# A block of gated delta rule and SwiGLU on one core: seven-product gate and up projections

## The reference

```python
x = x + ga * attn(layernorm(x) * (1 + ca) + sa)
h = layernorm(x) * (1 + cb) + sb
gate = einsum('bsd,hd->bsh', h, w_gate)      # hidden 2048
up = einsum('bsd,hd->bsh', h, w_up)
x = x + gb * einsum('bsh,dh->bsd', silu(gate) * up, w_down)
```

## Time and profile before

| | us |
|---|---|
| median of 3 runs (lowest, highest) | 1060.18 (1058.08, 1065.53) |
| the profiled execution | 1063.38 |
| its span | 1061.6 |
| TensorE busy (share) | 1022.6 (96%) |
| recurrence, about | 425 to 506 |
| feed-forward, about | 509 to 1059 |

### The profile page before, as it was taken

One profiled execution on the slowest core, in us unless ns is written; L12 is line 12 of the kernel. 1 busy time (PEld: TensorE's weight loads), 2 busy tenths in 40 slices (PEclk: granted clock), 3 DMA queues, 4 the chain that ended last, 5 costly groups with the idle time before them and its releaser, 6 DMA issues.

```text
span 1061.6 us, 20179 instructions
## 1 busy us (share of the span) xinstructions
PE 1022.6 (96%) x8112; PEld 822.1 (77%) x8112; DVE 626.2 (59%) x997; ACT 375.0 (35%) x685; POOL 225.8 (21%) x178
## 2 busy tenths in 40 slices
PE   6999999999998999998899999999999999999998
PEld 4676777777676888887777887888888888888886
DVE  5977377899855787878664333343333334334366
ACT  3676674445445343333453112211212212112110
POOL 1322530022025555554301000000000000004191
PEclk9999999999999999999999999999999999999999
DMA  6604336838256666775520001010100101001223
GB/s 212 196 14 135 73 80 165 247 100 215 64 125 170 141 153 146 188 187 130 174 72 28 1 1 60 1 60 1 33 28 1 60 1 58 2 0 70 80 80 119
DMA packets 153438, 97.42 MB, mean 92 GB/s; under 512 B 93569, under 2 KB 130689, under 8 KB 153217
## 3 DMA queue, kind: packets, MB, share of 16 engines
q1 hardware_dynamic: 153344, 96.12, 32.9%
HBM read 64.64 MB, written 31.46 MB: 91 GB/s over the span
## 4 chain that ended last, share of the span: by engine, by line
PE 73%; DVE 10%; DMA 5%; issue 4%; ACT 4%; SPq 4%; POOL 0%; DVEq 0%; ACTq 0%
PE ps L1302 70%; ACT t L1665 3%; PE ps L1310 3%; DVE t L1936 2%; DVE t L2046 2%; DMA scrU<-t 2%; SPq L1179 1%; DVE t L2034 1%; PE ps L1539 1%; DVE t L1941 1%; DVE t L2146 1%; DVE t L1946 1%; DMA scrA<-t 1%; SPq L1239 1%; DMA t<-scrA 1%
## 5 line engine op out<-in xcount | busy, mean ns | idle before, releaser
L1302 PE MATMUL ps<-t,t 128*128 128x512 f32 (+6 forms) x7292 | 969.7, 325 | 30.4 <-DVE t L1936 8.5
L1302 PEld LDWEIGHTS ps<-t,t 128*128 128x128 f32 (+4 forms) x7292 | 769.6, 159 | 215.1 <-issue 43.8
L1936 DVE TENSOR_TENSOR t<-ps,t 128x512 f32<-128x512 f32 (+2 forms) x288 | 199.6, 710 | 245.8 <-PE ps L1302 219.5
L1665 ACT ACTIVATE t<-t 128x512 fp32r<-128x512 f32 (+10 forms) x339 | 189.1, 579 | 308.8 <-DVE t L1936 206.2
L1936 DVE TENSOR_TENSOR t<-t,t 128x512 fp32r<-128x512 f32 (+14 forms) x210 | 168.1, 805 | 114.0 <-ACT t L1665 106.6
L1665 ACT ACTIVATE t<-ps 128x512 f32<-128x512 f32 (+5 forms) x202 | 109.1, 551 | 303.0 <-PE ps L1302 285.1
L2427 POOL TENSOR_TENSOR t<-t,t 128x512 f32<-128x512 f32 x16 | 22.5, 1408 | 375.2 <-DVE t L1936 373.1
L2046 DVE SCALAR_TENSOR_TENSOR t<-ps,t,t 128x511 f32<-128x511 f32 (+2 forms) x108 | 80.2, 747 | 3.3 <-ACT t L1665 0.5
L1665 ACT ACTIVATE t<-ps,t 128x512 f32<-128x512 f32 (+2 forms) x93 | 54.5, 617 | 26.1 <-PE ps L1310 13.0
L1310 PE MATMUL ps<-t,t 128*128 128x128 f32 (+1 forms) x340 | 52.3, 285 | 4.2 <-DVE t L1941 2.1
L1310 PEld LDWEIGHTS ps<-t,t 128*128 128x128 f32 (+1 forms) x340 | 38.1, 146 | 13.5 <-issue 5.5
(11 more groups left out here) (52 smaller groups left out, 257.2 us busy)
## 6 DMA issues: line engine op xcount, KB each, us to landing
scrU<-t SPq DMA_DIRECT2D x60, 256.0 KB, 2.9
t<-in_wf SPq DMA_DIRECT2D x16, 768.0 KB, 4.4
t<-scrU SPq DMA_DIRECT2D x32, 288.0 KB, 5.0
t<-scrU SPq DMA_DIRECT2D x32, 192.0 KB, 3.6
t<-in_W SPq DMA_DIRECT2D x19, 256.0 KB, 3.0
t<-in_x SPq DMA_DIRECT2D x16, 256.0 KB, 4.0
t<-in_wmod SPq DMA_DIRECT2D x4, 1024.0 KB, 6.3
t<-in_x SPq DMA_DIRECT2D x32, 128.0 KB, 2.9
```

Of the source, the lines that this page charges most:

```text
L1302: return e.matmul(o, l, r_, start=start, stop=stop, skip_group_check=True)
L1665: return e.activation(o, i, f, **kw)
L1936: return e.tensor_tensor(o, a, b, op)
```

## The change

Gate and up are made as seven products for two halves of hidden columns, of model columns and of tokens (two batches). An iteration `it` (0 to 15) is 256 hidden columns of one pair of batches: 0 to 7 are batches 0 and 1, 8 to 15 are 2 and 3. It has a gate pass and an up pass. A pass is seven products (`prod`, in order 0 to 6) of 6 matmuls of 512 columns (128 hidden columns, 256 model columns, 512 tokens of sums or differences). They go to three banks, 0 to 2 (gate) or 3 to 5 (up): products 0, 2, 4, 5 to the first, 1 to the second, 3 and 6 to the third. After products 0, 2 and 4 ScalarE copies the first bank to SBUF (`copy_s` 0, 1, 2) while it goes on accumulating; VectorE adds copies to banks (`cadd` 0, 1, 2). The first bank itself is the fourth result. Down products: eight token tiles `down(it, 0..7)` of the iteration before, 6 matmuls each; banks 6 and 7 in turn for them, for the late turns and for the gate rows.

Weights: gate, up (512 KB each, four quarters of 256 columns) and down (two of 256 KB) are loaded for every iteration, hence twice. GpSimd makes sums of quarters, four operations of 256 columns (`w_comb`), ScalarE the high parts in one operation of 7 × 256 columns (`w_high`), VectorE the low parts in one (`w_low_ff`). Down weights: high by ScalarE, low by GpSimd in four operations of 256 columns (`w_high_d`).

Tokens: batches 0 and 1 are turned straight from the recurrence, unit by unit (`turn_unit`, in slots 3, 4, 7, 8, 11, 12 and twice in 15; ScalarE modulates, eight operations a unit), 2 and 3 from scrN in iterations 1 and 2 (`turn_tile`); only these are stored to scrN. Sums of the token halves are made by GpSimd (`t_raw`) and VectorE (`t4`), the seven operands split by `split_h` (1024 columns; low parts on VectorE, in iteration 7 three of them on GpSimd). `late` holds the gated products, high and low parts (`gated`, `fh`, `fl`) that are put off to the next iteration. Results of batches 0 and 1 are finished and stored in iteration 8 (`post_0`, `add_0`, `store_0`), those of 2 and 3 at the end, as before.

The core of the diff:

```diff
+    NG = 8
+    GU = [(1, 0), (2, 1), (6, 0), (5, 2), (7, 0), (4, 0), (3, 2)]
+    A_OF = {1: 1, 2: 2, 6: 5, 5: 4, 7: 0, 4: 3, 3: 6}
+    B_OF = {1: 0, 2: 1, 6: 2, 5: 3, 7: 4, 4: 5, 3: 6}
...
+        p, free = take()
+        step("c_turn", u=u, bank=4 + 2 * p, free=[free])
+        t = tick("norm_tr")
+        unit_turned[u] = [t]
+        step("c_mod_unit", u=u, bank=4 + 2 * p, turned=t[1])
+        pfree(p, tick("a_cmod"))
...
+    def down(it, k):
+        i, free = ring_bank()
+        step("down", it=it, k=k, bank=i, free=free)
+        tick("down")
+        ring_free[i] = [tick("v_y")]
+        if it == 7:
+            step("post_0", k=k)
+        if it == 14:
+            step("out_pre", k=k)
...
+    split_h(0, 0, [("pr_kq", 16), ("v_kd", 16)])
+    w_low_ff(1, [("pr_kq", 16), ("v_kd", 16)])
+    t_raw(384, 512, [("a_cmod", 8)])
+    w_load(3, 0, [w_low_at[1]])
+    w_load(4, 1, done_r + [("v_ms", 16)])
+    step("po_sq", u=15)
+    prod(0, 0)
+    split_h(0, 1, done_r)
+    step("po_ln", u=15)
+    step("po_os", u=15)
+    prod(0, 1)
+    split_h(0, 2, done_r)
+    copy_s(0, 0)
+    ringed("po_tr", 15, ("v_oz", 16))
+    cadd(0, 0)
+    split_h(0, 3, done_r)
+    prod(0, 2)
+    split_h(0, 4, done_r)
+    step("po_yg", u=14)
+    step("po_add", u=14)
+    copy_s(0, 1)
+    prod(0, 3)
+    split_h(0, 5, done_r)
+    ringed("po_wo", 15, ("v_yg", 16))
+    split_h(0, 6, done_r)
+    step("po_stat", u=14)
+    step("po_xn", u=14)
+    prod(0, 4)
+    copy_s(0, 2)
+    step("po_yg", u=15)
+    step("po_add", u=15)
+    cadd(0, 1)
+    prod(0, 5)
+    prod(0, 6)
+    step("po_stat", u=15)
+    step("po_xn", u=15)
+    cadd(0, 2)
+    step("table", set="silu_and_others")
...
+    def next_gate(it, free):
+        w_high(gate_m(it + 1), free)
+        tok = w_low_ff(gate_m(it + 1))
+        if it < 14:
+            w_load(gate_m(it + 2), 0, [tok])
+
+    def iteration(it):
+        n, last, turn = 2 * it, it == 15, it == 7
+        if it:
+            prod(n, 0)
+            prod(n, 1)
+            copy_s(n, 0)
+            if it != 8:
+                flush()
+            prod(n, 2)
+            cadd(n, 0)
+            prod(n, 3)
+            copy_s(n, 1)
+            flush()
+            step("silu", it=it, t=0)
+            prod(n, 4)
+            if it != 8:
+                down(it - 1, 0)
+            copy_s(n, 2)
+            cadd(n, 1)
+            w_high(up_m(it), [("prod", 7 * (n - 1) + 7)])
+            step("silu", it=it, t=1)
+            w_load_next(it, w_low_ff(up_m(it)))
+            prod(n, 5)
+            prod(n, 6)
+            step("silu", it=it, t=2)
+            cadd(n, 2)
+            step("silu", it=it, t=3)
+            if it == 8:
+                down(7, 0)
+        if not last:
+            w_comb(gate_m(it + 1))
+        for k in range(1, 7):
+            if it and (it < 15 or k < 4):
+                down(it - 1, k)
+            if it in (1, 2) and k in (1, 2, 3, 4):
+                turn_tile(4 * it - 4 + k - 1)
+                if 4 * it + k - 3 < 8:
+                    step("load_xf", n=4 * it + k - 3)
+            if it == 3 and k in (2, 4):
+                gate_row(k // 2 - 1)
+            if it == 12 and k in (2, 4):
+                gate_row(k // 2 + 1)
+            if it and not last and k == 3:
+                next_gate(it, [("prod", 7 * n + 7)])
+        if not last and not turn:
+            w_comb(up_m(it + 1))
+        if it == 4:
+            t_raw(0, 512, [("a_cmod", 16), ("v_hs", 8), ("a_hs", 7)])
+        if last:
+            step("load_xo", ks=(6, 7))
+        if it == 8:
+            for k in range(4):
+                step("add_0", k=k)
+        n += 1
+        prod(n, 0)
+        if turn:
+            split_h(1, 0, [("prod", 7 * n + 1)])
+        prod(n, 1)
+        copy_s(n, 0)
+        if it == 0:
+            next_gate(0, [("prod", 7)])
+            step("silu", it=0, t=0)
+            step("silu", it=0, t=1)
+        if turn:
+            split_h(1, 1, [("prod", 7 * n + 2)], "p")
+        prod(n, 2)
+        cadd(n, 0)
+        if not turn:
+            gated(it, 0)
+        prod(n, 3)
+        copy_s(n, 1)
+        if not turn:
+            fh(it, 0)
+            fl(it, 0)
+        if it == 0:
+            step("silu", it=0, t=2)
+            step("silu", it=0, t=3)
+        if turn:
+            split_h(1, 2, [("prod", 7 * n + 3)])
+            split_h(1, 3, [("prod", 7 * n + 4)], "p")
+        prod(n, 4)
+        if it and not last:
+            down(it - 1, 7)
+        copy_s(n, 2)
+        cadd(n, 1)
+        if turn:
+            split_h(1, 4, [("prod", 7 * n + 5)])
+        else:
+            gated(it, 1)
+            w_high_d(it)
+            if it == 8:
+                for k in range(4, 8):
+                    step("add_0", k=k)
+            fh(it, 1)
+        prod(n, 5)
+        prod(n, 6)
+        if not turn:
+            gated(it, 2)
+            fh(it, 2)
+            cadd(n, 2)
+            gated(it, 3)
+            fl(it, 1)
+            fl(it, 2)
+        else:
+            split_h(1, 5, [("prod", 7 * n + 6)], "p")
+            split_h(1, 6, [("prod", 7 * n + 7)])
+            w_comb(up_m(it + 1))
+            cadd(n, 2)
+        if it == 8:
+            for k in range(8):
...
+        def rest():
+            if turn:
+                for t in range(4):
+                    gated(it, t)
+                    fh(it, t)
+                    if t == 1:
+                        w_high_d(it)
+                    fl(it, t)
             else:
-                held = [("v_y", at_y[(q - 1, b)] + s + 1)] if q else []
-            step("down", q=q, b=b, s=s, fs=fs, bank=down_banks[i], free=yb["free"][i], held=held, n=at_y[(q, b)] + s)
-            yb["free"][i] = [tick("v_y")]
-        done = ("down", count["v_y"])
-        for k, j, n in fs:
-            f_free[k] = [done]
-        if b == 3:
-            for k, j, n in fs:
-                gw_free[j % 4] = done
-
-    def late_norms():
-        todo = (8, 9, 10, 11, 12, 13, 14, 15)
-        for i, n in enumerate(todo):
-            mod(*turn(n), "av"[i % 2])
-            if i:
-                split(todo[i - 1], "pv"[i % 2])
-            yield
-        split(15, "p")
-        yield
-
-    nrm, tiles_at = late_norms(), [1, 1, 2, 0] * 3
-    pend = (0, 0, first_fs)
-    order_qb = [(0, 1), (1, 0), (1, 1), (0, 2), (0, 3), (1, 2), (1, 3)]
-    order_qb += [(q, b) for q in range(2, NG) for b in range(4)]
-    for q, b in order_qb:
-        fs = []
-        for done in products(q, b):
-            evict_gu(*done, fs)
-            for _ in range(tiles_at.pop(0) if tiles_at else 0):
-                next(nrm, None)
-        if (q, b) == (1, 1):
-            yb.update(ring=4, n=2)
-            yb["free"][2:] = [norm_free[norm_bank], norm_free[norm_bank + 1]]
-        if q == NG - 1:
-            for b_ in ((0, 1, 2), (3,), (), ())[b]:
-                step("load_xo", b=b_)
-            for s in range(4):
-                step("out_pre", b=b, s=s)
-        down(*pend)
-        pend = (q, b, fs)
-        if (q, b) == (0, 1):
-            step("split_ff", j=3)
-            step("load_ff", j=4, wait=("v_glo", 4))
-        if (q, b) == (1, 2):
-            step("split_ff", j=4, free=gw_free[0])
-            step("load_ff", j=5, wait=("v_glo", 5))
-            step("split_ff", j=5, free=gw_free[1])
-            for i in range(4):
-                y = yb["n"] % 4
-                yb["n"] += 1
-                step("gate_row", b=i, bank=down_banks[y], free=yb["free"][y])
-                yb["free"][y] = [tick("a_grow")]
-        if b == 1 and 2 <= q < NG - 1:
-            for j in (2 * q + 2, 2 * q + 3):
-                step("load_ff", j=j, wait=("v_glo", j))
-                step("split_ff", j=j, free=gw_free[j % 4])
-    down(*pend)
+                fh(it, 3)
+                fl(it, 3)
+        late.append(rest)
...
+                P_, bk = GU[o]
+                i, j = A_OF[P_], B_OF[P_]
+                if o == 0:
+                    e.wait_ge(*at_least(w_low_at[3 * it + up]))
+                    if n == 0:
+                        e.wait_ge(sem("a_dl"), 16)
+                    elif n == 1:
+                        e.wait_ge(sem("v_os"), 16)
+                    else:
+                        e.wait_ge(sem("v_gf" if up else "a_si"), 4 * (it - 1) + 3)
+                elif o == 1:
+                    if n == 1:
+                        e.wait_ge(sem("v_yg"), 16)
+                    elif n > 1:
+                        e.wait_ge(sem("v_c"), 3 * (n - 2) + 1)
+                elif o == 3:
+                    if n == 0:
+                        e.wait_ge(sem("v_os"), 16)
+                    elif n > 1:
+                        e.wait_ge(sem("v_c"), 3 * (n - 2) + 3)
+                elif o == 6:
+                    e.wait_ge(sem("v_c"), 3 * n + 2)
+                else:
+                    e.wait_ge(sem("a_sp"), 3 * n + {2: 1, 4: 2, 5: 3}[o])
+                first = it % 8 == 0 and not up
```

(52 more changed lines are left out.)

722 lines of the change are left out of this document (386 added, 336 removed).

## The result

The changed kernel takes 1095.05 us (median of 4 runs, 1093.9 to 1096.71), the kernel before 1060.43 beside it: ratio 1.0321, 95% interval 1.028 to 1.0361. The forecast was 1061.2 with a range up to 1078; the kernel is 3.2% slower. The profiled execution took 1095.81 us with a span of 1093.8, 32.2 more than before; its mean granted clock is 0.977, and 0.995 before.

A forecast was written before the change was run, and what follows sets the result against it. The prediction took the number of TensorE matmuls to bound the kernel. Its terms, −43.5 + 9.2 + 12.9 + 3.5 + 11 + 4 + 1 + 2.9 + 0 = +1.0 us, added to the median 1060.18, gave 1061.2 us, range 1045 to 1078.

The forecast's parts named there:

- −43.5 for the matmuls: Gate and up passes: 192 matmuls fewer at 0.2267 us each save 43.5 us if TensorE never waits.
- Product 6 behind a down's eviction: Gate and up passes: product 6 waits for cadd 1, queued behind a down's eviction; 0.33 us 28 times, +9.2 us.
- Down 6, w_low_ff between two evictions: Down 6 needs down 4's bank, whose eviction stands behind w_low_ff; 0.92 us 14 times, +12.9 us.
- the port: VectorE's w_low_ff can meet GpSimd's w_comb on the shared port; 0.25 us 14 times, +3.5 us, bounds 0 to 10.5.
- The recurrence: Six turns of batches 0 and 1 in recurrence slots cost 0.48 us each; +2.9 us, bounds 2 to 6.
- Iterations 1 and 2: Eight late turns cost 3.8 us and their waits, each holding a bank, 2.3; counted within the entry's zero sum.
- The turn: From batches 0 and 1 to 2 and 3, iterations 7 and 8: late high parts, gating chain, locks; +11 us, bounds 7 to 16.
- The entry: From rec_o's end to the second iteration, set by VectorE: 40.4 us; with late turns change 0, bounds −8 to +8.
- The end: Product 5 without a down, late first evictions and slower final operations beside out_pre; +4 us, bounds 2 to 8.
- A: Rival: waits are covered better and the entry gains; total −13 us, 1047 us; chance 0.22.
- B: Rival: the port between VectorE and GpSimd costs the full 0.75 us 14 times, and more elsewhere; 1077 us; chance 0.18.
- C: Rival: the entry alone is late by its bound of 8 us; 1069 us; chance 0.10.

The follow-up runs named there:

- e8: Changed kernel with the order edits of e1, e2, e5, e6 and e7 together: 1049.63 us, ratio 0.9884 to the kernel before.
- e6: Changed kernel with copy_s 2 and cadd 1 put before down 0 (down 7 in the up pass): 1092.78 us, ratio 1.0293 to the kernel before.
- e5: Changed kernel with next_gate behind down 6 instead of down 3 from iteration 3 on: 1080.2 us, ratio 1.0162 to the kernel before.
- e4: Changed kernel with the first of w_comb's four GpSimd sums made four times: 1098.03 us, ratio 1.0349 to the kernel before.
- e1: Changed kernel with the modulates of a turned unit put behind po_sq of the next slot: 1084.53 us, ratio 1.0208 to the kernel before.
- e3: Changed kernel with 15 matmuls nobody reads put ahead of down 5 in iterations 1 and 2: 1092.18 us, ratio 1.0284 to the kernel before.
- e2: Changed kernel with next_gate behind down 6 instead of down 3 in iterations 1 and 2: 1089.48 us, ratio 1.0264 to the kernel before.
- e11: e8 with, in iteration 0's up pass, next_gate behind copy 1 and silus 2 and 3 behind cadd 1: 1046.59 us, ratio 0.9851.
- e7: Changed kernel with tiles 1 to 3 of iteration 7 and silu 0 put behind cadd 1 in iteration 8's gate pass: 1094.43 us, ratio 1.0302.
- e9: e8 with w_high_d of iteration 7 put behind product 4 of its up pass: 1052.55 us, ratio 0.9913 to the kernel before.

## Why the prediction was wrong

- **−43.5 for the matmuls: right.** In e8, where the visible waits of the steady stretch are gone, an iteration takes 30.4 us for 29.92 without any wait.
- **Product 6 behind a down's eviction, 9.2: right**, nearly: 0.50 an iteration measured in e6 for 0.66.
- **Down 6, w_low_ff between two evictions, 12.9, and the port, 3.5: right** in the steady stretch. e5 takes both away, and the iteration falls by 1.17 us (31.91 to 30.74) for 0.92 + 0.25 forecast. The port's part is 0.33 of it: the mean wait of nine is 0.93, and 0.60 where w_low_ff is undisturbed. e4 sets a bound on what more of it would cost. That gate rows and turns move the wait to down 5 I had overlooked.
- **The recurrence, +2.9 (2 to 6): wrong, +13.1.** The step that failed: "what TensorE needs of it, po_tr, comes only after 66 matmuls of 5.38 us". It is true of po_tr. But I followed the delayed po_sq only to the matmuls that read its result, and not to VectorE's queue behind it, in which po_yg's eviction frees the banks of pr_exp. Six such slots last 1.8 us longer than in e1 (14.05 and 12.23), 10.9 in all, and e1 leaves nothing of the excess (170.5 us for 170.6 forecast). 10 us of the miss.
- **Iterations 1 and 2, 2.3 for the waits of the late turns and 0.92 each for down 6: wrong, 13.7 more.** The step that failed: the two were added as if independent, with a down (1.36 us) as cover between the delayed eviction and the matmuls that need its bank. They form one chain: the modulates delay ScalarE's high part, that delays w_low_ff, that the eviction, and a late turn holds the other bank meanwhile, so that the cover is gone. 3.40 us idle, twice, and 5.3 us of clock behind it (e3), together 11.5 us (e2). Most of the other 2.2 is the clock behind the wait of 2.73 at 555.26, 0.67 from 556 to 560: 66 matmuls in 17.19 us, where e11, with 0.48 of wait there, has 60 in 14.04, which for 66 would be 15.4.
- **The turn, +11 (7 to 16): 15.4**, within its bounds. The idle of 8.23 us was forecast at 6.9; the 2.61 at 836.05 was not, and e5 shows it to be next_gate again. e7 and e9 only moved the other hole, so what limits the turn stays open.
- **The entry, 0 (−8 to +8): +2.2**, within. The forecast summed VectorE's queue as a whole; in the trace TensorE waits 3.01 us at 526.02 and 2.73 at 555.26, and from 528 to 536 it runs at 0.50. e11 takes 3.0 of it back.
- **The end, +4: right**, 58.25 us from down 6 of iteration 14 to the last matmul for 57.7. t_raw's +1 no run singles out.
- **The test that I named was too weak.** TensorE's idle time from iteration 1 on is 532 − 497.2 = 34.8 us by the window below, inside the 20 to 45 that I had called consistent. The loss hid in the recurrence and in busy time at half the clock. Periods and stage lengths would have told, a sum of idle time doesn't.

```profile
558.00:1090.00 532.00, 497.16 (x2075) 387.92 (x2073) 343.26 (x393) 210.12 (x314) 226.15 (x214) 0.98 0.18 60
```

- **The rivals:** A needed covers that weren't there; B is ruled out by e4 and by the 0.33 us an iteration above; C's place is right only in small part. None had the recurrence or iterations 1 and 2. My bounds treated the terms as independent, each around a steady iteration, whereas the cost arose where two moved things met in one queue.

What stays open: why the low clock follows some waits and not others of the same length. A part of what stages with the same code differ by from one profiled execution to the next, up to 4 us, is that: of the 3.75 us in e2, 2.6 are there when the recurrence starts, and 1.4 come in one of its slots (426.63 to 442.11, 15.48 us for 14.05), with 0.59 granted from 436 to 440.
